# A chain of graph and mixture layers on one core: ScalarE's splits ahead of the gathered copies, and the last pass's turned rows in a tile of their own

## The reference

```
# first mixture (L1_ffn): 8 experts of width 1536, two chosen per row, and a shared one
logits = xf @ w_router.T
scores = softmax(logits);  _, top_idx = top_k(scores + expert_bias, 2)
routed = sum over e of comb[:, e] * (silu(xf @ wg.T) * (xf @ wu.T)) @ wd.T
out    = routed + shared expert(xf)
# second mixture (L3_ffn): 8 experts of width 3072, two chosen per row, no shared one;
# its result is the last thing added to x, which is then the output
```

## Time and profile before

| | |
|---|---|
| median of three runs | 1283.53 us (1280.08 to 1284.25) |
| the profiled execution's own time | 1283.21 us |
| its span | 1281.4 us |
| TensorE matmul busy | 1143.3 us, 89% of the span |
| VectorE busy | 496.3 us, 39% |
| ScalarE busy | 384.7 us, 30% |
| moved by DMA | 443.77 MB, mean 346 GB/s over the span |
| chain that ended last | TensorE 51%, DMA 33%, VectorE 10%, ScalarE 4%, issue 2% |

### The profile page before, as it was taken

One profiled execution on the slowest core, in us unless ns is written; L12 is line 12 of the kernel. 1 busy time (PEld: TensorE's weight loads), 2 busy tenths in 40 slices (PEclk: granted clock), 3 DMA queues, 4 the chain that ended last, 5 costly groups with the idle time before them and its releaser, 6 DMA issues.

```text
span 1281.4 us, 15594 instructions
## 1 busy us (share of the span) xinstructions
PE 1143.3 (89%) x6431; PEld 692.4 (54%) x6431; DVE 496.3 (39%) x805; ACT 384.7 (30%) x442; POOL 22.1 (2%) x47
## 2 busy tenths in 40 slices
PE   5999999888899998878899779989899998998888
PEld 4677686667735453446755544545445445544533
DVE  6977542446821231223623433233223123312310
ACT  5766312233721231222213152223123123312310
POOL 2000000000000000000000000000000000000000
PEclk9999999999999999988999899999999999999899
DMA  9988646737699999999401099999999999999996
GB/s 376 423 336 340 269 160 252 303 148 287 255 400 426 424 426 425 426 423 426 175 17 42 32 427 425 424 426 424 425 426 425 425 425 426 426 426 425 425 426 259
DMA packets 43301, 443.77 MB, mean 346 GB/s; under 512 B 4848, under 2 KB 5008, under 8 KB 8672
## 3 DMA queue, kind: packets, MB, share of 16 engines
q1 hardware_dynamic: 40320, 427.05, 80.0%
q0 software_dynamic: 2912, 15.74, 3.2%
HBM read 442.38 MB, written 0.39 MB: 346 GB/s over the span
## 4 chain that ended last, share of the span: by engine, by line
PE 51%; DMA 33%; DVE 10%; ACT 4%; issue 2%; SPq 0%; POOL 0%; DVEq 0%; ACTq 0%
DMA ring<-in_weights 19%; DMA scratch<-in_weights 10%; PE PJ L1662 8%; PE AC L1688 5%; PE TP L1709 5%; PE AC L1481 4%; DMA extra<-in_weights 3%; PE PJ L1649 3%; PE PJ L1651 3%; PE PJ L1650 3%; PE AC L1493 3%; PE PJ L1397 2%; PE MS L1374 2%; DVE ring_lo L1142 2%; PE PJ L1454 1%
## 5 line engine op out<-in xcount | busy, mean ns | idle before, releaser
L1662 PE MATMUL PJ<-ring,picked 128*32 128x512 f32 (+1 forms) x900 | 199.6, 599 | 6.9 <-DMA ring<-in_weights 6.0
L1662 PE MATMUL PJ<-scratch,picked 128*64 128x512 f32 (+1 forms) x444 | 107.0, 594 | 0.9 <-DMA scratch<-in_weights 0.9
L1662 PEld LDWEIGHTS PJ<-ring,picked 128*32 128x32 f32 (+1 forms) x900 | 58.2, 123 | 91.0 <-issue 90.5
L1142 DVE TENSOR_TENSOR ring_lo<-ring,w_lo_u 128x1536 fp32r<-128x1536 f32 x36 | 62.1, 1755 | 105.5 <-ACT w_lo_u L756 105.4
L1124 DVE SCALAR_TENSOR_TENSOR act<-low,CB,PJ 128x512 f32<-128x512 f32 x48 | 35.7, 744 | 140.4 <-PE PJ L1651 96.4
L739 ACT ACTIVATE low<-PJ 128x512 f32<-128x512 f32 x48 | 28.4, 591 | 202.0 <-PE PJ L1662 150.5
L1142 DVE TENSOR_TENSOR ring_lo<-ring,w_hi_u 128x1536 fp32r<-128x1536 f32 x32 | 55.1, 1755 | 86.6 <-ACT w_hi_u L756 86.5
L1662 PE MATMUL PJ<-extra,picked 128*32 128x512 f32 (+1 forms) x384 | 85.7, 595 | 2.4 <-DMA extra<-in_weights 1.4
L1709 PE MATMUL TP<-scratch,extra 128*32 128x512 f32 (+3 forms) x528 | 85.8, 487 | 1.7 <-issue 1.7
L1709 PE MATMUL TP<-ring,extra 128*64 128x512 f32 (+2 forms) x496 | 80.5, 487 | 1.0 <-issue 1.0
L756 ACT ACTIVATE w_hi_u<-ring 128x1536 fp32r<-128x1536 f32 x32 | 46.3, 1483 | 114.6 <-DMA ring<-in_weights 101.8
(11 more groups left out here) (375 smaller groups left out, 1899.0 us busy)
## 6 DMA issues: line engine op xcount, KB each, us to landing
ring<-in_weights SPq DMA_DIRECT2D x156, 1536.0 KB, 30.8
scratch<-in_weights SPq DMA_DIRECT2D x79, 1536.0 KB, 32.7
extra<-in_weights SPq DMA_DIRECT2D x34, 1536.0 KB, 34.1
extra<-in_attn POOLq DMA_DIRECT2D x12, 768.0 KB, 9.3
extra<-in_attn POOLq DMA_DIRECT2D x6, 512.0 KB, 7.6
extra<-in_weights SPq DMA_DIRECT2D x8, 384.0 KB, 24.9
scratch<-in_ffn_vectors POOLq DMA_DIRECT2D x1, 2688.5 KB, 12.2
extra<-in_x SPq DMA_DIRECT2D x1, 384.0 KB, 3.0
```

What stands on the lines that cost most here:

```text
L1142: v.tensor_tensor(slab_lo(n)[:, half * HALF:(half + 1) * HALF], half_slab(n, half), hi_half(n, half).bitcast(F32), ALU.subtract).then_inc( ...
L1662: ins = mm(dst[c], x[:, t, c], slab_at(LOAD[q, kind, side])[:, t * SEG:(t + 1) * SEG], start=(t == 0), stop=(t == KT - 1))
```

## The change

It has six parts.

1. On ScalarE in the first mixture, the copy of `gather(0)` goes from behind `silu_of(0)` to behind the splits of g and u of pass 1, and the copy of `gather(2)` from right behind that of `gather(1)` to behind the splits of g and u of pass 2.
2. `keep_warm(10, PJ[:, 0:P])` is issued on TensorE behind the router's product, in both mixtures.
3. `count_chosen`, which in the first mixture is issued inside `up("g", 0)`, goes from before its fifth tile to before its third.
4. The last pass's two d slabs are loaded in two parts each in place of four, and `down(47)` waits before its first and third quarter.
5. In the second mixture `turn_hidden(47)` goes from behind `down(46)` to before it.
6. ScalarE copies the turned rows of pass 47 to `low[1]` and not to `hT`, which `down(46)` still reads.

The few words that came with the change also speak of the first mixture's full passes being spread evenly to its end. The table of passes is the same in both kernels.

```diff
--- before.py
+++ after.py
@@ -386,6 +386,12 @@
                 return (wh if s % 2 == 0 else wl)["dgu"[(s - RING) // 2]][:]
             return extra_lo[:, s - 2 * RING, :]
 
+        def hT_of(q):
+
+            if q == LAST_PASS[3]:
+                return low[1]
+            return hT if PASSES[q][0] == "pair" else hTh
+
         def hi_half(n, half):
             return (wh if HI[n] % 2 == 0 else wl)["u"][:, half * HALF:(half + 1) * HALF]
 
@@ -498,9 +504,9 @@
                         closing.append((n, expert[rank] * (3 * m["per"]) + (m["slab"] + 3 * j + kind)))
                         continue
                     slab(n, expert[rank] * (3 * m["per"]) + (m["slab"] + 3 * j + kind))
-                for t in range(4):
+                for t in range(2):
                     for n, index in closing:
-                        part = slice(t * D, (t + 1) * D)
+                        part = slice(t * HALF, (t + 1) * HALF)
                         sp.dma_start(slab_at(n)[:, part], weights[index, :, part]) \
                             .then_inc(S(f"closing_landed_{t}"), 16)
 
@@ -740,7 +746,7 @@
 
                 def hidden_turned(q):
                     act.wait_ge(S("pe_t"), q + 1)
-                    A(hT if PASSES[q][0] == "pair" else hTh, TP[:, 0:SEG], ACT.Copy).then_inc(S("hT_ready"), 1)
+                    A(hT_of(q), TP[:, 0:SEG], ACT.Copy).then_inc(S("hT_ready"), 1)
 
                 def whole_hi(q, kind, both=(0, 1)):
 
@@ -775,17 +781,18 @@
                 for q in range(m["first"], LAST_PASS[l] + 1):
                     whole_hi(q - 1, "d")
                     silu_of(q)
-                    if l == 1 and q == 0:
-                        gather(0)
                     if q > m["first"]:
                         hidden_turned(q - 1)
                     if l == 1 and q == 1:
                         gather(1)
-                        gather(2)
                     if l == 1 and q == 2:
                         shares_turned()
                     whole_hi(q + 1, "g")
                     whole_hi(q + 1, "u")
+                    if l == 1 and q == 0:
+                        gather(0)
+                    if l == 1 and q == 1:
+                        gather(2)
                 whole_hi(LAST_PASS[l], "d")
                 hidden_turned(LAST_PASS[l])
 
@@ -1598,6 +1605,7 @@
                 if l == 1:
                     ins = bias_row(MS[:, 8:16], ROW_MIXED, MIXED_EB, MIXED_EB + E8, start=True, stop=True)
                 ins.then_inc(S("router_product"), 1)
+                keep_warm(10, PJ[:, 0:P])
 
                 def count_chosen():
 
@@ -1640,7 +1648,7 @@
                         pe.wait_ge(S("tokens_lo"), nth + 1)
                         n = LOAD[q, kind, 0]
                         for t in range(KT):
-                            if between and t == 4:
+                            if between and t == 2:
                                 between()
                             half, w = t // 3, slice(t % 3 * SEG, (t % 3 + 1) * SEG)
                             hi, lo = hi_half(n, half), slab_lo(n)[:, t * SEG:(t + 1) * SEG]
@@ -1702,11 +1710,11 @@
                         else:
                             pe.wait_ge(S("gathered"), 3 * nth + 3)
                     for t in range(4):
-                        if q == LAST_PASS[3]:
-                            pe.wait_ge(S(f"closing_landed_{t}"), 32)
+                        if q == LAST_PASS[3] and t % 2 == 0:
+                            pe.wait_ge(S(f"closing_landed_{t // 2}"), 32)
                         for a, b in halves():
                             for side, c in columns(q):
-                                ins = mm(Y[c, a:b], hT[:, t * P:(t + 1) * P][:, c],
+                                ins = mm(Y[c, a:b], hT_of(q)[:, t * P:(t + 1) * P][:, c],
                                          slab_at(LOAD[q, "d", side])[:, t * D + a:t * D + b],
                                          start=(j == 0 and t == 0), stop=(t == 3 and j == m["per"] - 1),
                                          skip_group_check=True)
@@ -1745,11 +1753,14 @@
                     up("u", q)
                     if l == 1 and q == 0:
                         gather(0)
+                    if l == 3 and q == end:
+                        turn_hidden(end)
                     if q > first:
                         down(q - 1)
                     if l == 1 and q == 1:
                         gather(2)
-                turn_hidden(end)
+                if l == 1:
+                    turn_hidden(end)
                 if complete(end - 1):
                     add_pair(end - 1)
                 down(end)
```

## The result

The changed kernel takes 1270.72 us, the median of 4 runs (1269.96 to 1271.52), against 1283.89 us (1280.08 to 1285.68, 4 runs) for the kernel before, timed with it: a ratio of 0.9901, with a 95% interval of 0.9878 to 0.9925. The forecast was 1273.3 in a range of 1269 to 1279.5. The profiled execution took 1269.96 us with a span of 1268.2 us, 13.2 us less than before, where the sum had 10.0.

The account below looks back on a forecast made before the run. TensorE's progress through passes 0 to 2 was taken to set the weight stream's start; 3.1 + 4.2 + 1.4 + 0 + 1.3 = 10.0 us off 1283.2 gave 1273.2, forecast as 1273.3, range 1269 to 1279.5.

Parts of the forecast that it names:

- The bound: First mixture: TensorE's way through passes 0 to 2 sets the stream's start; each us won there moves everything behind by one.
- The first pause: TensorE's 4.23 us wait before pass 1: shrinks to about 2.2 us, with pass 1 starting 3.1 us earlier.
- the count: VectorE's 1.14 us wait for TensorE's count of chosen experts, before pass 1: goes whole, giving 1.1 us.
- The second pause: TensorE's 4.16 us wait before pass 2, for VectorE's low part: goes whole, 4.2 us in the sum.
- new wait: Rival, chance 0.11: VectorE's unbroken chain is late for down(0) or pass 2, so part of the gain goes; 1276 to 1279.
- the rival in which it holds the stream: Rival, chance 0.04: the load into slot 13 waits for the third gathered copy, delaying all slabs behind it; 1291 us.
- The clock of pass 2: Pass 2's g product runs at full clock once no wait precedes it, 4.27 us in place of 5.67: 1.4 us.
- The clock of pass 1: Pass 1 stays slow behind its shortened wait: 0 taken, 1.4 us as the other end, giving 1271.9.
- the 342.6 to 344 that had been named: Sign in the profile after: SyncE's load that ended the stream's pause is issued then, in place of 352.63 us.
- The fill: Ten matmuls behind the router's product in both mixtures: 1.2 us at full clock, fitting the idle time; 0 gain, 1 us loss allowed.
- The end: Last pass: transposes hide in the wait before down(46), so down(47) starts at 1269.25, not 1270.54; gain 1.3 us, low end 0.5.
- the 2 us either way: Allowance on the total, since every pause behind shifts against the clock's phase and each slow product costs 1.4 us or not.

Follow-up runs that it names:

- the pair of delays: Changed kernel with 32 needless TensorE matmuls added before the g product of pass 2 (1276.86 us) or, separately, of pass 12 (1267.37 us).
- the splits alone: Kernel before with only ScalarE's splits put ahead of the gathered copies in the first mixture: 1272.96 us, ratio 0.9931.

## Why the prediction was right, point by point

**The bound.** Right, and shown by the pair of delays: what TensorE wins before the load at 352.63 moves everything behind it, and inside the stream it wins nothing. One reading of the earlier trace rows was wrong, without harm. SyncE's waits in the kernel before, in two windows (columns: waited for, us in total, times, longest), 262 to 300 us and then 345 to 353.4 us:

```profile
SPq L495 <- DVE sid L1189: 23.5, 1, 23.5
...
SPq L464 <- PE AC L1688: 12.5, 1, 12.5
```

From 280 to 294 us SyncE did not stand before a slot that TensorE holds: it waited for VectorE's order of the experts. The pause that counts is the second, and that one is ended by TensorE's down product.

**The first pause: 3.1 us forecast, 3.15 measured.** The mechanism was as told: 1.88 us from the copy's place, and VectorE's shares next in line, which putting them off confirmed. What was given to the count (1.1 us) holds only in a kernel without the fill. In this one the two do the same work twice.

**The second pause: 4.2 forecast, 4.16 measured.** It went whole with both copies moved, and stayed whole with the first alone. VectorE kept ahead of TensorE, so no new wait took its place, and the copy that was to be 0.2 us late is 0.1 us late (315.75 behind the gather's end at 315.66). It comes 4.7 us earlier than before, so the rival in which it holds the stream had nothing to stand on.

**The clock of pass 2: 1.4 forecast, 1.4 measured.**

**The clock of pass 1: 0 taken, 1.6 measured.** This is the term of the sum that was mis-sized, and the main part of the 3.2 us that the forecast was short. It was read from the pause of 2.16 us before slow matmuls at the end. Here a pause of 2.33 us was followed by 4.23 us of full clock. One row was too little to read it from. Pass 1 had a pause of 2.33 to 2.37 us in eight kernels of this case, and seven of them ran at the full clock; the very pause at the end that the term was read from, 2.15 or 2.16 us in seven kernels, was followed by 5.37 us in five and by 7.04 or 7.06 in two, and the kernel before was one of the two. The other end, 1.4, had been named, and with it the sum was 1271.9. That the load came at 342.09, just ahead of the 342.6 to 344 that had been named, is this term.

**The fill: 0 forecast, 0 measured in the changed kernel, by a wrong reading.** Fourteen rows of such matmuls are seven fills, so ten take 2.50 us and do not fit in 1.58. The price was right only because VectorE's low part sets the second half of u of pass 0, which the prediction had as its reserve. On the kernel before, where the count stands later, the fill alone has a ratio of 0.9985, or 1.9 us (0.8 to 3.2).

**The end: 1.3 forecast, 1.4 to 1.5 measured.** Right in its mechanism. The landings were no bound with four parts or with two.

**The middle: not in the forecast, 1.25 measured.** The g product of pass 17 took 581.45 - 574.63 = 6.82 us before and 569.69 - 563.89 = 5.80 after: 1.0 of the 1.25 us is TensorE's clock in one product whose code did not change. It is the 2 us either way that were allowed for, and that it fell on the good side is luck: no part of the change acts on pass 17. It also carried the second mixture's first load 11.8 us forward, past the 8 to 10 that had been named.

Together 3.15 + 4.16 + 1.4 + 1.6 + 1.25 + 1.4 = 13.0 of the 13.2 us.

## What to carry to other kernels

An engine that issues in order makes everything behind a waiting instruction wait too: where a copy waits for a product, look at what stands behind it that does not need it, and what the next engine does with that. Before counting a wait as won, look whether the DMA stream is held at that point or runs full behind it: the same 7.3 us on TensorE cost 6 to 7 us before the stream's start and nothing inside. And the next change is named by what is late once the wait is gone: here VectorE's shares, about 4 us more.

## What the runs showed of the hardware

The same pause does not always bring the lower clock. Pass 1 was preceded by 2.33 to 2.37 us of idleness in eight kernels. Its g product took 4.22 to 4.24 us in seven of them, and 307.81 - 302.02 = 5.79 us with the first copy alone, with PEclk 0.58 from 302 to 306 us. What decides between them the runs don't show. Nor is the price of a slow product one figure: behind pauses of 4.16 to 4.23 us the g product took between 5.67 and 6.83 us, where it takes 4.25 at the full clock.

In consequence a stretch of unchanged code is not constant. From the load that ends the pause to the second mixture's first load it was 376.1 to 380.3 us over the twelve kernels in which nothing of TensorE's work there differs but the ten fills behind the second router, and 375.9 us in the one with work added at pass 12. With the splits alone the g product of pass 17 took 570.05 - 565.79 = 4.26 us and down(17) with what follows 593.51 - 585.16 = 8.35; in the kernel after 5.80 and 9.91. That is 3.1 us between two kernels with the same code there, twice what the end's edit gives, and whoever judges a small edit at the far end by the total alone measures this.

A fill, a matmul of the identity in f32, shows as two rows of the timeline: 32 fills are x64, at 114 to 116 ns a row. So does a product of a pair pass, 12 matmuls as x24. The products in split precision, with operands of type fp32r, show as one row each.
